# Fused attention and FFN layer: weight loads for the next head pair issued one pair earlier, V weights in two staging buffers

## The chip, the cores and the metric

The kernel runs on the 8 cores of one Trainium2 chip, each core with one of the 8 sequences of the batch. The metric is device microseconds of the slowest core, median of several runs.

## The reference

Each core computes one transformer layer on x of 4096 tokens by 1024 features: causal self-attention with 16 heads of 64, projection, residual and layer norm, then an FFN (1024 to 4096, exact GELU, back to 1024), residual and layer norm. Cut to what matters here:

```python
qkv = x @ c_attn_kernel.T + c_attn_bias          # c_attn_kernel: [3*1024, 1024], float32
q, k, v = jnp.split(qkv, 3, axis=2)              # then 16 heads of 64
scores = jnp.einsum('bqhd,bkhd->bhqk', q * scale, k) + causal_bias
attn = jnp.einsum('bhqk,bkhd->bqhd', softmax(scores), v).reshape(b, s, d)
x = layernorm(x + attn @ c_proj_kernel.T + c_proj_bias)
x = layernorm(x + gelu(x @ w1 + b1) @ w2 + b2)
```

## The kernel before

The program has three stages with a barrier between them: attention, projection with the first layer norm, FFN with the second. The change is in the first.

**Pairs and units.** Heads are worked on in 8 pairs (`NPAIR`). A pair's loop has 144 units: query tile g of 512 tokens (g from 0 to 7) against key block j of 128 tokens, 4(g+1) blocks for tile g. For a unit TensorE computes the scores of two heads (L762), ScalarE the exponential (L792; L808 for the four blocks on the diagonal, which VectorE then masks, L818), TensorE multiplies by V (L837). The scores of the next unit are issued ahead of this unit's product with V. At the end of a tile VectorE copies the sums out (L856), and the tile's tail begins: the row of softmax sums goes to DRAM and back into 128 partitions on SyncE's queue, VectorE takes the reciprocal (L711), it goes to DRAM again, GpSimd loads it as a broadcast (`rb<-r_s`) and multiplies (L736, L742). `flush_tail` places a tail two tiles later, and the last two at the end of the pair. After them stands the store of the pair's result (`attn_s<-arena`).

**The next pair's preparation.** While pair p-1 is computed, Q, K and V of pair p are prepared. `make_start(p)` builds a list of small pieces (thunks): load 128 rows of the Q and of the K weights with a cast from float32 to bfloat16 (`t_wld`, GpSimd's queue), transpose them on TensorE (`t_wtr`, L351) and copy them out (L359), then the Q and K projections (`t_qk`, L379, L389, L396) with a norm bound (`t_nrm`, L436, L449), and at last a bias column (`t_cb`, L498, L507). For even p the list goes on with V for the pairs p and p+1: two loads of 128 rows (`t_vld`), their transposes (`t_vtr`, L540) and copies (L548), and the V projection per key block (`mk_vg`, L562, L572, L579, copied out by L600 and L607). Odd pairs need no V work.

A thunk with a negative number is run as soon as it heads the list and takes no unit's place; of the others each unit from the ninth on takes one. So the Q and K loads of pair p are written into unit 0 of loop p-1, their transposes into units 8 and 9, and the V loads just ahead of their transposes, at about units 59 and 60. Loop 1 in the text below is the loop over pair 0, loop 2 that over pair 1, and so on.

**Order and waits.** Each engine executes its own instructions in the order in which this program adds them, and an instruction waits for the semaphores of what it depends on. GpSimd runs ahead of TensorE where nothing stops it: a load written just ahead of its transposes can be issued much earlier in time. Loads with a cast are issued by GpSimd alone. They land in `wcastA`, 3072 columns: two slabs of 1024 for Q and K, one for V, which the second V load (r = 1) can fill only once the first slab has been transposed and copied out:

```python
            def t_vld(r):
                stg = wcastA[:, 2048:3072]
                if r >= 1:
                    dep_stage = H_["vwtr"][r - 1]
```

**The prologue.** Before the first loop, x is loaded in 16 tiles of 256 tokens into two staging buffers (`xstage_b`, 4096 columns, not used afterwards), transposed on TensorE (L641) and copied into `xT` (L649); between them the thunks of pair 0 run as far as their numbers allow.

In the trace's names `arena` is the one large buffer in on-chip memory of which all of these are parts, `ps` is the accumulator memory, `wqkv` the Q, K and V weights in DRAM. DMAs of GpSimd all have line L239, those of SyncE L231.

Of the kernel before, what the change touches and what calls it, by code (L numbers as in the profile page):

```python
# [13 lines left out]
D = 1024  # L14
FF = 4096
NPAIR = 8
# [87 lines left out]
def build_nc(S=4096, debug_taps=False):  # L104
    NTG = S // TGA
    NKT = S // 128
    NTT = S // 128
# [5 lines left out]
    wqkv_d = nc.dram_tensor("wqkv", [3 * D, D], F32, kind="ExternalInput").ap()  # L113
# [120 lines left out]
    def gp_dma(stream, outs_ins, deps=(), tag=""):  # L234
        sem = sch._sem(stream)

        def em():
            for o, i in outs_ins:
                gp.dma_start(out=o, in_=i).then_inc(sem, 16)  # L239
        return sch.add("pool", em, deps, tag, n_dma=len(outs_ins), sem=stream)  # L240
# [45 lines left out]
    xstage_b = bf(A_xstage, 4096)  # L286
    last_ev = {0: None, 1: None}
    xT_ready = [None] * NTT

    xTb = xT  # L290
    wcastA = bf(A_wcast, 3072)
# [13 lines left out]
    qsq_user = [None, None]  # L305
    pending_vevs = {}
    handles = [None] * NPAIR

    def make_start(p):
        pb = p % 2  # L310
# [21 lines left out]
        thunks = []  # L332
# [3 lines left out]
        def t_wld(wi):  # L336
            row0 = [128 * p, D + 128 * p][wi]
            stg = wcastA[:, 1024 * wi : 1024 * wi + 1024]
            dep_stage = handles[p - 1]["wtr"][wi] if p > 0 else None
            ld = gp_dma(f"pw{wi}", [(stg, wqkv_d[row0 : row0 + 128, :])],  # L340
                        (dep_stage,), f"wld{p}.{wi}")
            H_["wld"].append(ld)

        def t_wtr(wi):
            wdstT = [H_["wqT"], H_["wkT"]][wi]
            stg = wcastA[:, 1024 * wi : 1024 * wi + 1024]
            bki = 4 + wi % 2
            def em_wtr(stg=stg, bki=bki):
                r = None
                for k in range(8):  # L350
                    r = t.transpose(  # L351
                        bank_bf(bki)[:, 128 * k : 128 * k + 128],
                        stg[:, 128 * k : 128 * k + 128],
                        idb,
                    )
                return r
            tr = sch.add("pe", em_wtr, (H_["wld"][wi], bank45_user[wi % 2]), f"wT{p}.{wi}")
            def em_wev(wdstT=wdstT, bki=bki):
                return v.tensor_copy(wdstT, bank_bf(bki)[:, 0:1024])  # L359
            ev = sch.add("dve", em_wev, (tr,), f"wTev{p}.{wi}")  # L360
            H_["wev"].append(ev)
            H_["wtr"].append(tr)
            bank45_user[wi % 2] = ev

        for wi in range(2):
            thunks.append((-1, lambda wi=wi: t_wld(wi)))
        for wi in range(2):
            thunks.append((0, lambda wi=wi: t_wtr(wi)))

        def t_qk(qi, g):  # L370
            wT = [H_["wqT"], H_["wkT"]][qi]
# [141 lines left out]

        thunks.append((NKT - 1, t_cb))

        if p % 2 == 0:
            wvg = bf(A_wvT, 2048)
            va_next = bf(A_va + ((p + 1) % 3) * 2 * 65 * NKT, 2 * 65 * NKT)
            va3_next = va_next.rearrange("p (h a c) -> p h a c", h=2, a=NKT, c=65)
            vevs_next = pending_vevs[p + 1]  # L520
            vstate = {"wld": []}

            def t_vld(r):
                row0 = 2 * D + 128 * p + 128 * r
                stg = wcastA[:, 2048:3072]
                if r >= 1:
                    dep_stage = H_["vwtr"][r - 1]
                else:
                    dep_stage = handles[p - 2]["vwtr"][1] if p >= 2 else None
                ld = gp_dma("pw2", [(stg, wqkv_d[row0 : row0 + 128, :])],  # L530
                            (dep_stage,), f"vwld{p}.{r}")
                vstate["wld"].append(ld)

            def t_vtr(r):
                stg = wcastA[:, 2048:3072]
                bki = 4 + r % 2
                def em_wtr(stg=stg, bki=bki):
                    rr = None
                    for k in range(8):
                        rr = t.transpose(  # L540
                            bank_bf(bki)[:, 128 * k : 128 * k + 128],
                            stg[:, 128 * k : 128 * k + 128],
                            idb,
                        )
                    return rr
                tr = sch.add("pe", em_wtr, (vstate["wld"][r], bank45_user[r % 2]), f"vwT{p}.{r}")
                def em_wev(r=r, bki=bki):
                    return v.tensor_copy(  # L548
                        wvg.rearrange("p (f pr c) -> p f pr c", f=8, pr=2, c=128)[:, :, r, :],
                        bank_bf(bki).rearrange("p (a c) -> p a c", a=8, c=128),  # L550
                    )
                ev = sch.add("dve", em_wev, (tr,), f"vwTev{p}.{r}")
                H_["vwtr"].append(ev)
                bank45_user[r % 2] = ev
# [39 lines left out]
            def mk_vg_b(a):  # L594
# [17 lines left out]
                bank45_user[par] = ev2  # L612
                vevs_next.append(ev2)

            thunks.append((-1, lambda: t_vld(0)))
            thunks.append((0, lambda: t_vtr(0)))
            thunks.append((-1, lambda: t_vld(1)))
            thunks.append((1, lambda: t_vtr(1)))
            for a in range(NKT):
                thunks.append((a, lambda a=a: mk_vg(a)))  # L620
                thunks.append((a, lambda a=a: mk_vg_b(a)))
# [4 lines left out]
    for tp_ in range(NTT // 2):  # L626
        b_ = tp_ % 2
        stg = xstage_b[:, 2048 * b_ : 2048 * b_ + 2048]
# [37 lines left out]
    for p in range(NPAIR):  # L666
        H_ = handles[p]
# [862 lines left out]
```

How the kernel before makes its waits and increments, by code:

```python
    def emit_engine(self, name, eng):  # L80
        sems = self.sems
        wm = {}
        for op in self.ops:
            if op.eng != name:
                continue
            for d in op.deps:
                if d.eng == "pe" and name == "pe":
                    continue
                v = d.val
                if wm.get(d.sem, 0) >= v:
                    continue
                eng.wait_ge(sems[d.sem], v)
                wm[d.sem] = v
            last = op.emit()
            if not op.is_dma:
                assert last is not None, f"op {op.tag} returned no instruction"
                last.then_inc(sems[op.sem], 1)
        if name == "pool":
            for sname, val in sorted(self.final.items()):
                if val > 0 and sname not in ("pe", "act", "dve"):
                    eng.wait_ge(sems[sname], val)
# [127 lines left out]
        def em():  # L229
            for o, i in outs_ins:
                sp.dma_start(out=o, in_=i).then_inc(sem, 16)
# [5 lines left out]
        def em():  # L237
            for o, i in outs_ins:
                gp.dma_start(out=o, in_=i).then_inc(sem, 16)
```

## Time and profile before

| | us |
|---|---|
| median of 3 runs | 3476.89 |
| lowest, highest of the 3 | 3474.47, 3582.14 |
| the profiled execution's own time | 3474.0 |
| its span on the slowest core (7) | 3472.5 |
| spans of cores 0, 1, 2, 3 | 3453.8, 3466.9, 3470.2, 3461.1 |
| spans of cores 4, 5, 6, 7 | 3454.7, 3471.2, 3458.3, 3472.5 |
| busy on core 7: TensorE, ScalarE | 2757.3, 1655.8 |
| busy on core 7: VectorE, GpSimd | 758.7, 305.6 |

The profiled execution is one run; its span goes from the first to the last instruction of the slowest core. Busy time is the sum over an engine's instructions, and a busy TensorE is not TensorE at its peak, since matmuls overlap in its pipeline. The attention loops lie at about 180 to 2120 us.

### The profile page before, as it was taken

How to read it: one execution, taken by the hardware profiler on the slowest of the kernel's cores; microseconds unless marked ns; L12 is line 12 of the kernel's file. 1: busy time of each engine (PE TensorE's matmuls, PEld its weight loads, DVE VectorE, ACT ScalarE, POOL GpSimd, SP SyncE). 2: the span in 40 equal slices, each digit the busy share in tenths (PEclk: the TensorE clock that was granted, in tenths of full speed). 3: DMA queues.
4: the chain of work that ended last, by engine and by line, in shares of the span. 5: the costliest groups of instructions: out<-in, count | busy, mean ns of one | idle time of the engine just before them, and what ended most of it. 6: DMA issues, size and time to landing. Idle time of an engine off the chain costs nothing.

```text
span 3472.5 us, 42144 instructions; the slowest of 8 cores (3453.8 to 3472.5 us)
## 1 busy us (share of the span) xinstructions
PE 2757.3 (79%) x14609; PEld 1222.6 (35%) x14609; DVE 758.7 (22%) x2136; ACT 1655.8 (48%) x1969; POOL 305.6 (9%) x383
## 2 busy tenths in 40 slices
PE   5687687888687787788787673577689999999997
PEld 2432123322123222223221111222456656566664
DVE  3442132232232242242231210233000000000000
ACT  0046745647655647546558783255133343433433
POOL 1000110010110110100111111111200000000000
PEclk9899998989898899899899996788899999999998
DMA  4200100010100100100100003865721111111110
GB/s 75 48 7 10 25 17 10 10 28 7 28 13 10 28 10 7 31 10 10 28 10 10 26 10 88 178 235 187 154 53 55 37 55 31 43 50 37 55 31 25
DMA packets 88204, 155.16 MB, mean 45 GB/s; under 512 B 26208, under 2 KB 50944, under 8 KB 85952
## 3 DMA queue, kind: packets, MB, share of 16 engines
q0 software_dynamic: 32736, 100.69, 11.6%
q1 hardware_dynamic: 55264, 51.78, 5.4%
q8 instruction: 124, 2.03, 0.2%
q14 instruction: 80, 0.66, 0.1%
HBM read 135.14 MB, written 50.86 MB: 54 GB/s over the span
## 4 chain that ended last, share of the span: by engine, by line
PE 62%; DMA 11%; ACT 9%; issue 9%; DVE 7%; POOL 1%; DVEq 0%; ACTq 0%; SPq 0%; POOLq 0%
PE ps L1306 12%; PE ps L1255 12%; PE ps L837 11%; ACT arena L792 7%; PE ps L762 7%; PE ps L389 4%; PE ps L379 3%; DMA arena<-x 3%; PE ps L974 3%; DMA arena<-w 2%; PE ps L572 2%; PE ps L562 2%; DMA rb<-r_s 2%; DMA arena<-wqkv 2%; PE ps L436 1%
## 5 line engine op out<-in xcount | busy, mean ns | idle before, releaser
L792 ACT ACTIVATE arena<-ps,cbt 128x1024 bf16<-128x1024 f32 x896 | 979.5, 1115 | 489.7 <-PE ps L762 488.5
L837 PE MATMUL ps<-arena 128*65 128x512 bf16 x2304 | 740.6, 405 | 221.2 <-DVE arena L818 90.6
L1255 PE MATMUL ps<-arena 128*128 128x256 bf16 x4096 | 539.6, 276 | 42.1 <-ACT arena L1276 23.6
L1306 PE MATMUL ps<-arena 128*128 128x512 bf16 x2048 | 532.7, 383 | 45.1 <-DVE stats L1368 28.1
L1276 ACT ACTIVATE arena<-ps,b1f 128x256 bf16<-128x256 f32 x512 | 238.8, 476 | 603.7 <-PE ps L1306 568.4
L1255 PEld LDWEIGHTS ps<-arena 128*128 128x128 bf16 x4096 | 402.7, 99 | 209.7 <-issue 60.7
L762 PE MATMUL ps<-arena 64*128 64x512 bf16 x2304 | 468.3, 404 | 0.0
L837 PEld LDWEIGHTS ps<-arena 128*65 128x65 bf16 x2304 | 183.3, 113 | 498.1 <-issue 467.6
L808 ACT ACTIVATE arena<-ps,cbt 128x1024 bf16<-128x1024 f32 (+3 forms) x256 | 200.5, 795 | 256.8 <-PE ps L762 256.8
L762 PEld LDWEIGHTS ps<-arena 64*128 64x128 bf16 x2304 | 110.4, 93 | 510.5 <-issue 510.4
L1306 PEld LDWEIGHTS ps<-arena 128*128 128x128 bf16 x2048 | 199.7, 99 | 190.4 <-issue 59.4
L1338 DVE SCALAR_TENSOR_TENSOR arena<-ps,arena 128x512 f32<-128x512 f32 x64 | 40.4, 688 | 919.0 <-PE ps L1316 919.0
L818 DVE TENSOR_TENSOR arena<-arena,masks_s 128x128 bf16<-128x128 bf16 x512 | 99.3, 234 | 611.1 <-ACT arena L808 595.5
L974 PE MATMUL ps<-arena 128*128 128x512 bf16 x512 | 136.4, 414 | 66.3 <-DVE arena L995 65.4
L239 POOL DMA_DIRECT2D rb<-r_s x64 | 35.7, 557 | 1570.9 <-DMA r_s<-rowf 1570.9
L416 DVE CAST arena<-ps 128x512 bf16<-128x512 f32 x128 | 88.6, 692 | 358.7 <-PE ps L396 358.7
L379 PE MATMUL ps<-arena 128*128 128x512 bf16 x512 | 140.4, 399 | 23.4 <-DVE arena L649 11.8
L389 PE MATMUL ps<-arena 128*128 128x512 bf16 x512 | 135.5, 388 | 0.0
L1019 ACT ACTIVATE arena<-arena 128x1024 f32<-128x1024 f32 x32 | 33.8, 1058 | 195.2 <-PE ps L1157 112.7
L436 PE MATMUL ps<-arena,ones_bf 128*1 128x512 bf16 x128 | 50.7, 396 | 95.9 <-DVE arena L427 95.9
L449 DVE TENSOR_REDUCE stats<-ps 1x1 f32<-1x512 f32 x128 | 86.9, 679 | 83.3 <-PE ps L436 83.3
L736 POOL TENSOR_TENSOR arena<-arena,rb 64x512 bf16<-64x512 f32 x64 | 80.4, 1256 | 203.6 <-DMA rb<-r_s 203.6
(96 smaller groups left out, 1582.5 us busy)
## 6 DMA issues: line engine op xcount, KB each, us to landing
rb<-r_s POOLq DMA_DIRECT2D x64, 256.0 KB, 3.6
arena<-x SPq DMA_DIRECT2D x8, 2048.0 KB, 10.9
x_s<-arena POOLq DMA_DIRECT2D x8, 2048.0 KB, 7.8
arena<-x_s SPq DMA_DIRECT2D x16, 1024.0 KB, 6.5
out<-arena POOLq DMA_DIRECT2D x16, 1024.0 KB, 8.5
arena<-x POOLq DMA_DIRECT2D x16, 512.0 KB, 7.1
attn_s<-arena POOLq DMA_DIRECT2D x8, 1024.0 KB, 5.2
arena<-attn_s SPq DMA_DIRECT2D x64, 128.0 KB, 11.1
```

What stands on the lines that cost most here:

```text
L379: r = t.matmul(bank(bki), wT[:, 128 * fc : 128 * fc + 128], xTb[:, S * fc + TGA * g : S * fc + TGA * g + TGA], start=(fc == 0), stop=False,)
L389: t.matmul(bank(bki), wT[:, 128 * fc : 128 * fc + 128], xTb[:, S * fc + TGA * g : S * fc + TGA * g + TGA], start=False, stop=False,)
L416: return v.tensor_copy(dst[:, TGA * g : TGA * g + TGA], bank(bki))
L762: r = t.matmul(PS[:, 1024 * ub + 512 * hh : 1024 * ub + 512 * hh + 512], k2[64 * hh : 64 * hh + 64, 128 * j : 128 * j + 128], q2[64 * hh : ...
L792: return sc.activation(Pb, quad, AF.Exp, bias=cbcol, scale=0.125)
L808: return sc.activation(Pb.rearrange("p (h c) -> p h c", h=2, c=512)[:, :, dcol:], quad.rearrange("p (h c) -> p h c", h=2, c=512)[:, :, dcol:],
L818: r = v.tensor_tensor(Pb[:, 512 * hh + dcol : 512 * hh + dcol + 128], Pb[:, 512 * hh + dcol : 512 * hh + dcol + 128], masks[:, 0:128], ALU ...
L837: r = t.matmul(PS[0:65, 3072 + 512 * hh : 3584 + 512 * hh], va[:, 65 * (NKT * hh + j) : 65 * (NKT * hh + j) + 65], Pb[:, 512 * hh : 512 * ...
L974: r = t.matmul(bank(bki), atg[:, TGA * fc + 128 * tc : TGA * fc + 128 * tc + 128], wpT[:, 1024 * fc + 512 * oh : 1024 * fc + 512 * oh + 51 ...
L1255: r = t.matmul(bank(bki)[:, 0:TGC], w1sb[:, FF * fc + 128 * hc : FF * fc + 128 * hc + 128], x2Tt[:, TGC * fc : TGC * fc + TGC], start=(fc ...
L1276: lambda hc=hc, hb=hb, htile=htile: sc.activation(htile, bank(F1BANKS[hb])[:, 0:TGC], AF.Gelu, bias=b1f[:, hc : hc + 1]),
L1306: r = t.matmul(bank(2 + 2 * tc + oh), htile[:, 128 * tc : 128 * tc + 128], w2sb[:, 1024 * hc + 512 * oh : 1024 * hc + 512 * oh + 512], sta ...
```

## The change

For Q and K, `t_wld` is now used for pair 0 alone. Every list puts, right behind the two transposes of its pair, two loads for the pair after it (`t_wld_next`) into the same two slabs; each waits for the transposes that read its slab. For V, the two loads of pairs 2, 4 and 6 are now written at the very head of the list before (`t_vld_next`, in the lists of pairs 1, 3 and 5), and go to the two halves of `xstage_b`, which is free after the prologue; they wait for the V transposes two pairs before to have been copied out. Pair 0's V loads stay as they were. TensorE's, VectorE's and ScalarE's instructions keep their order; only the buffers that L540 reads in pairs 2, 4 and 6 change.

```diff
         def t_wld(wi):
...
-            dep_stage = handles[p - 1]["wtr"][wi] if p > 0 else None
             ld = gp_dma(f"pw{wi}", [(stg, wqkv_d[row0 : row0 + 128, :])],
-                        (dep_stage,), f"wld{p}.{wi}")
+                        (), f"wld{p}.{wi}")
             H_["wld"].append(ld)
+
+        def t_wld_next(wi):
+            row0 = [128 * (p + 1), D + 128 * (p + 1)][wi]
+            stg = wcastA[:, 1024 * wi : 1024 * wi + 1024]
+            ld = gp_dma(f"pw{wi}", [(stg, wqkv_d[row0 : row0 + 128, :])],
+                        (H_["wtr"][wi],), f"wld{p + 1}.{wi}")
+            wld_pending[p + 1].append(ld)
...
-        for wi in range(2):
-            thunks.append((-1, lambda wi=wi: t_wld(wi)))
+        if p == 0:
+            for wi in range(2):
+                thunks.append((-1, lambda wi=wi: t_wld(wi)))
+        else:
+            H_["wld"] = wld_pending.pop(p)
         for wi in range(2):
             thunks.append((0, lambda wi=wi: t_wtr(wi)))
+        if p + 1 < NPAIR:
+            wld_pending[p + 1] = []
+            for wi in range(2):
+                thunks.append((-1, lambda wi=wi: t_wld_next(wi)))
...
+        if p % 2 == 1 and p + 1 < NPAIR:
+            vld_pending[p + 1] = []
+
+            def t_vld_next(r):
+                row0 = 2 * D + 128 * (p + 1) + 128 * r
+                stg = xstage_b[:, 1024 * r : 1024 * r + 1024]
+                if p + 1 == 2:
+                    dep = (handles[0]["vwtr"][1], xT_ready[NTT - 1])
+                else:
+                    dep = (handles[p - 1]["vwtr"][r],)
+                ld = gp_dma("pw2" if r == 0 else "pw3",
+                            [(stg, wqkv_d[row0 : row0 + 128, :])],
+                            dep, f"vwld{p + 1}.{r}")
+                vld_pending[p + 1].append(ld)
+
+            for r_ in (1, 0):
+                thunks.insert(0, (-1, lambda r=r_: t_vld_next(r)))
...
-            vstate = {"wld": []}
+            vstate = {"wld": [] if p == 0 else vld_pending.pop(p)}
...
             def t_vtr(r):
-                stg = wcastA[:, 2048:3072]
+                if p == 0:
+                    stg = wcastA[:, 2048:3072]
+                else:
+                    stg = xstage_b[:, 1024 * r : 1024 * r + 1024]
...
-            thunks.append((-1, lambda: t_vld(0)))
-            thunks.append((0, lambda: t_vtr(0)))
-            thunks.append((-1, lambda: t_vld(1)))
-            thunks.append((1, lambda: t_vtr(1)))
+            if p == 0:
+                thunks.append((-1, lambda: t_vld(0)))
+                thunks.append((0, lambda: t_vtr(0)))
+                thunks.append((-1, lambda: t_vld(1)))
+                thunks.append((1, lambda: t_vtr(1)))
+            else:
+                thunks.append((0, lambda: t_vtr(0)))
+                thunks.append((1, lambda: t_vtr(1)))
```

Where loads move, on GpSimd. In the prologue, the difference (rows with + are new); `arena<-x` are the tiles of x, `arena<-wqkv` slabs of weights, and the words in brackets the semaphores waited for (`sem_pe` TensorE, `sem_dve` VectorE):

```order
 L239 DMA arena<-x 128x2x1024 [waits sem_spc,sem_dve,sem_pbias,sem_pe]
 L239 DMA arena<-wqkv 128x1024 x2
+L239 DMA arena<-wqkv 128x1024 [waits sem_pe] x2
 L239 DMA arena<-x 128x2x1024
 L239 DMA arena<-x 128x2x1024 [waits sem_dve] x14
 L239 DMA arena<-wqkv 128x1024
```

The Q and K loads of pair 1 have moved ahead of the second tile of x, and wait there for TensorE's transposes of pair 0's slabs.

At the head of the second loop, and about its 60th unit, GpSimd before: the end of the tail of pair 0, the store, then the Q and K loads of pair 2; further down the two V loads, one on each side of a tile's tail:

```order
L742 TENSOR_TENSOR arena<-arena,rb 64x512
L239 DMA attn_s<-arena 128x4096 [waits sem_pool]
L239 DMA arena<-wqkv 128x1024 [waits sem_pe] x2
L239 DMA rb<-r_s 64x1024 [waits sem_sr0]
```

```order
L742 TENSOR_TENSOR arena<-arena,rb 64x512
L239 DMA arena<-wqkv 128x1024 [waits sem_dve]
L239 DMA rb<-r_s 64x1024 [waits sem_sr1,sem_pool]
L736 TENSOR_TENSOR arena<-arena,rb 64x512 [waits sem_pl1]
L742 TENSOR_TENSOR arena<-arena,rb 64x512
L239 DMA arena<-wqkv 128x1024 [waits sem_dve]
L239 DMA rb<-r_s 64x1024 [waits sem_sr0,sem_pool]
```

The same engine in the changed kernel, from the last loads of the prologue to the first tail of the first loop (the third row holds pair 0's second V load and pair 2's first):

```order
L239 DMA arena<-x 128x2x1024 [waits sem_dve] x14
L239 DMA arena<-wqkv 128x1024
L239 DMA arena<-wqkv 128x1024 [waits sem_dve] x2
L239 DMA arena<-wqkv 128x1024
L239 DMA arena<-wqkv 128x1024 [waits sem_pe] x2
L239 DMA rb<-r_s 64x1024 [waits sem_sr0]
```

Both V loads of pair 2 and its Q and K loads are now on the queue ahead of every tail of the first loop. In the second loop the place behind the store holds the Q and K loads of pair 3, and no V load stands among its tails.

## Rows read from the trace of the kernel before

**Rows 1.** The page, section 1: busy us (share of the span) xinstructions.

```profile
PE 2757.3 (79%) x14609; PEld 1222.6 (35%) x14609; DVE 758.7 (22%) x2136; ACT 1655.8 (48%) x1969; POOL 305.6 (9%) x383
```

**Rows 2.** List of waits, core 7: us in total, times, longest.

```profile
PE ps L540 <- DMA arena<-wqkv: 51.2, 4, 15.2
PE ps L351 <- DMA arena<-wqkv: 46.8, 7, 8.2
PE ps L641 <- DMA arena<-x: 10.4, 2, 8.9
```

**Rows 3.** Timeline, head of loop 2: start, us, engine, line, operation [idle before <-releaser].

```profile
413.76 1.03 PE L837 MATMUL ps<-arena 128*65 128x512 bf16 x2 [4.67 <-DVE arena L818]
...
425.28 1.26 POOL L742 TENSOR_TENSOR arena<-arena,rb 64x512 bf16<-64x512 f32 x1
...
427.69 1.09 POOL L239 DMA_DIRECT2D arena<-wqkv  x2
...
436.20 1.01 PE L351 MATMUL ps<-idb_s,arena 128*128 128x128 bf16 x8 [8.11 <-DMA arena<-wqkv]
...
445.07 1.22 DVE L856 COPY arena<-ps 65x1024 f32<-65x1024 f32 x1
```

**Rows 4.** Timeline, the two V loads and their transposes in loop 2.

```profile
513.54 0.60 POOL L239 DMA_DIRECT2D arena<-wqkv  x1
...
540.08 0.62 PE L540 MATMUL ps<-idb_s,arena 128*128 128x128 bf16 x8
...
553.59 0.60 POOL L239 DMA_DIRECT2D arena<-wqkv  x1
...
557.73 1.01 PE L540 MATMUL ps<-idb_s,arena 128*128 128x128 bf16 x8 [15.20 <-DMA arena<-wqkv]
...
560.24 1.12 ACT L792 ACTIVATE arena<-ps,cbt 128x1024 bf16<-128x1024 f32 x1 [16.48 <-PE ps L762]
```

**Rows 5.** Timeline, the transposes of the Q weights in loop 1.

```profile
201.47 0.62 PE L351 MATMUL ps<-idb_s,arena 128*128 128x128 bf16 x8
```

**Rows 6.** Stretches: us, busy of PE, PEld, DVE, ACT, POOL, granted clock, DMA share, GB/s.

```profile
420.40:428.10 7.70, 6.22 (x16) 1.17 (x16) 1.45 (x3) 4.29 (x4) 3.94 (x5) 0.56 0.12 37
436.10:441.00 4.90, 4.80 (x25) 2.35 (x26) 2.50 (x6) 0.69 (x1) 0.00 (x0) 0.50 0.03 6
540.90:542.50 1.60, 1.54 (x4) 0.29 (x4) 1.03 (x2) 0.47 (x1) 0.00 (x0) 0.50 0.01 5
557.70:561.30 3.60, 3.57 (x18) 1.91 (x18) 0.69 (x1) 1.06 (x1) 0.00 (x0) 0.52 0.02 5
1214.00:1450.00 236.00, 185.07 (x754) 51.21 (x754) 63.62 (x159) 146.55 (x144) 26.54 (x27) 0.91 0.06 17
2200.00:2450.00 250.00, 151.93 (x751) 61.96 (x749) 76.71 (x274) 108.98 (x136) 43.14 (x78) 0.79 0.66 205
2450.00:3472.00 1022.00, 931.05 (x6208) 607.09 (x6208) 60.53 (x272) 361.28 (x672) 26.87 (x46) 0.97 0.19 50
```

**Rows 7.** Timeline, the prologue's loads and transposes, and pair 0's second V transposes.

```profile
9.03 0.74 POOL L239 DMA_DIRECT2D arena<-x  x1 [5.80 <-DVE b1f L280]
...
10.84 0.73 POOL L239 DMA_DIRECT2D arena<-x  x1
...
16.99 1.86 PE L641 MATMUL ps<-idb_s,arena 128*128 128x128 bf16 x16 [8.95 <-DMA arena<-x]
...
21.90 1.01 PE L351 MATMUL ps<-idb_s,arena 128*128 128x128 bf16 x8 [2.12 <-DMA arena<-wqkv]
...
24.37 1.87 PE L641 MATMUL ps<-idb_s,arena 128*128 128x128 bf16 x16 [1.46 <-DMA arena<-x]
...
143.89 1.01 PE L540 MATMUL ps<-idb_s,arena 128*128 128x128 bf16 x8 [5.68 <-DMA arena<-wqkv]
```

**Rows 8.** List of waits, core 2.

```profile
PE ps L540 <- DMA arena<-wqkv: 50.3, 4, 15.2
PE ps L351 <- DMA arena<-wqkv: 41.2, 8, 7.0
```

More of the change, by code:

```diff
@@ L307, in build_nc @@
     handles = [None] * NPAIR
+    wld_pending = {}
+    vld_pending = {}
     def make_start(p):
@@ L525, in t_vld @@
                 stg = wcastA[:, 2048:3072]
[L526 to L529, printed above, removed]
+                dep_stage = H_["vwtr"][r - 1] if r >= 1 else None
                 ld = gp_dma("pw2", [(stg, wqkv_d[row0 : row0 + 128, :])],
```

## The prediction, made before the changed kernel was run

> **What bounds the kernel now.** I read the page first, then the list of waits, then the timeline around each wait that the change touches, then granted clock by stretch, then the cores. The page's first section has TensorE busy for 79% of the span and no other engine above 48% [rows 1]; TensorE executes strictly in the order written, so while it waits no attention work is done. The question is how much of its idle time hangs on the weight loads that the change moves. The list of waits answers: the transposes of the V weights (L540) waited 51.2 us for `arena<-wqkv` in 4 waits, those of the Q and K weights (L351) 46.8 us in 7 waits [rows 2]. The change can touch only these 98.0 us.
>
> Where do they lie? The program has 8 pairs of heads, and each loop over a pair also prepares the next. For Q and K the timeline of the second loop shows it: GpSimd normalises the last tile of the previous pair (L742, from 425.28), issues the store of that pair's result, and only then the two loads, at 427.69. TensorE waits 8.11 us, from about 428.1, and starts the transposes at 436.20 [rows 3]. So these loads are late because they stand on GpSimd's queue behind the tail of the previous pair, not because the data would be slow. In the first loop, which has no earlier pair, the same transposes begin at 201.47 with no wait [rows 5]: this is what the changed kernel should look like in all loops. For V the first of two loads was issued at 513.54, 26 us ahead, and its transposes at 540.08 did not wait. The second waits for the first one's buffer and stands behind a normalisation; it is issued at 553.59, lands 4.1 us later, and TensorE has stood 15.20 us. ScalarE stood beside it, 16.48 us until the next scores came [rows 4]. Nothing else filled the gap, so the stalls are on the path.
>
> **The change part by part.** The sum is made against the profiled run, 3474.0 us (span 3472.5 on core 7, 1.5 around it). The median of the three runs shown is 3476.9, 2.9 above it.
>
> Early Q/K loads, loops 2 to 7. The program's 7 waits of L351 hold one in the prologue, 2.12 us [rows 7], which stays, since that load is not moved. The other six are 46.8 - 2.1 = 44.7 us. In the changed kernel these loads are issued a whole pair earlier (some 235 us), behind transposes that are done by then: -44.7.
>
> Early V loads, pairs 2, 4, 6. Of the 4 waits of L540 the first, 5.68 us at 143.89 [rows 7], belongs to pair 0 and stays (its load goes out as before, with less behind it; I count nothing, since a load alone took 4.1 us too [rows 4]). The other three are 51.2 - 5.7 = 45.5 us. They go whole, since each V slab now has a buffer of its own: -45.5. Next late after the second transposes is VectorE's copy of them, as before; 0 to 3 us over three places, taken as 0.
>
> TensorE's clock. In the stretch behind the Q/K stall, 436.1 to 441.0, TensorE was granted 0.50 of its clock, that is 1.2 instead of 2.4 GHz, with 4.80 us busy; behind the V stall, 557.7 to 561.3, 0.52 with 3.57 us busy [rows 6]. At the full clock that work takes half: 2.4 us saved in each of six places and 1.8 in each of three, 19.8 in all, if the clock is full there once the stalls are gone. Against it: it was already at 0.56 in 420.4 to 428.1, ahead of the stall, and at 0.50 in 540.9 to 542.5 [rows 6]. So the low stretch would partly only move. Bounds 0 and -20; I take the middle, -10.
> The Trainium skill, TensorE: Matmul & The Clock Gate (Part 1: The HAM clock gate), says that the throttled clock is the default and that only activity lifts it, which makes all of the slow work behind a stall a cost of the stall. By that rule the sum has -20 here. The trace agrees that a stall is followed by the low level, but also shows the low level in a stretch where TensorE was busy 6.22 of 7.70 us.
>
> Cost in the prologue. The two Q/K loads of pair 1 now stand on GpSimd's queue ahead of the second tile of x, and wait for the transposes of pair 0's weights. Before, the second x load was issued at 10.84 and its transposes started at 24.37. Now it can go only after the transposes that start at 21.90 and take 1.0, plus 0.6 for issuing the last weight load: at 23.5. All 14 later x loads are queued behind it, and TensorE's next work behind x. The first x load took 9.03 to 16.99, 7.96 us, with nothing ahead of it [rows 7]: 23.5 + 7.96 - 24.37 = +7.1. Lower bound: in a filled queue x came only about 2.5 us after the weight load ahead of it (21.90 to 24.37), 23.5 + 2.5 - 24.37 = +1.6. Upper: that 2.5 once more for the weight load now just ahead, +9.6. I take +7. It cannot be a gain. The later x loads have time to catch up: only two of the 16 were ever waited for, the first and the second [rows 2, 7].
> The Trainium skill, DMA: Bandwidth & Descriptors (Anatomy of one DMA), puts a load at about 2 us plus its bytes at 436 GB/s. For 1 MB of x that is an estimated 4.4 us and the term would be +3.5. The row has 7.96 for the same load, and the row is used.
>
> In the loops, the moved loads' waits block GpSimd only until the transposes of the same loop; what stands behind them is the first tile's 1/sum broadcast, which waits for its own chain anyway: 0.
>
> The slowest core. Core 7 loses the most from these waits, 98.0 us; core 2 has 91.5 [rows 8], with a span of 3470.2 against 3472.5. If its prologue parts are like core 7's, core 2 ends at 3470.2 - (91.5 - 7.8) = 3386.5 before the other terms, core 7 at 3472.5 - 90.2 = 3382.3. The end may pass to core 2: bounds 0 and +4, taken +3.
>
> Sum: 3474.0 - 44.7 - 45.5 - 10 + 7 + 3 = 3383.8, so 3384 us, 2.7% below the median before.
>
> **The rivals.**
> 1. The clock comes back whole (-20 for -10): 3374. For it: the low level stands right behind each stall. Against: it is also there ahead of two of them.
> 2. A new wait takes the place: with TensorE 8 us earlier at the head of a pair, it meets the tail of the previous one. The next such need is VectorE's copy of the second tile (L856, at 445.07), which needs the normalisation that ended at 426.54; it would come at about 437, 10 us too late to wait [rows 3]. For it: at 413.76 TensorE did stand 4.67 us in such a tail [rows 3]. If each of six loops gave that back: 3384 + 28 = 3412, no change by the measurement.
> 3. The prologue costs more, since x stays behind and the clock falls there too: twice the upper bound, +19 instead of +7: 3396.
> 4. Slower: denser work on all cores lowers the granted clock of the attention loops. In 1214 to 1450 it was 0.91 with TensorE busy 185 of 236 us; in 2200 to 2450, another stage, 0.79 [rows 6]. Estimated over the 1812 us from 138 to 1950 that is 1421 us busy; at 0.79 they would take 15% more, +216, so 3600. It decides below 0.854, where 93 us of gain are used up. Against it: the last stage is denser still, 931 of 1022 us, and was granted 0.97 [rows 6].
> 5. The loads are early but TensorE still waits, because the wait was for something else. Against: the first V load, issued early, had no wait [rows 4]. It would give 3474 + 7 = 3481.
>
> **How the numbers follow.** Forecast 60%, rival 1 15%, rival 2 8%, rival 3 11%, rival 4 2%, rival 5 4%. Low end: 3474.0 - 90.2 - 20 + 2 = 3366, high end: 3474.0 - 90.2 + 0 + 10 + 4 + 3 (copies) = 3401, plus the 2.9 between the profiled run and the median and a little of rival 2: 3405. A measurement of this kernel can tell 2% from no change, which is 3407. Forecast, rivals 1 and 3 lie beyond it, 86%, and a part of rival 2: 0.87 faster; the rest of rival 2 and rival 5, 0.11 the same; rival 4, 0.02 slower.
>
> **What would show it.** In the profile after, the waits of L351 and L540 for `arena<-wqkv` should fall from 98.0 to about 8 us (the prologue's only), in 2 or 3 waits; loops 2 to 7 should each be about 8 us shorter, those with V work about 23. The start of the second x transposes should move from 24.37 to about 31. If granted clock right behind the old stall places is full, the clock term is nearer to 20. I am wrong if TensorE waits at the heads of pairs for L856 or L818 grow by more than 10 us in sum, if the prologue grows by more than 10 us, or if the mean granted clock of the loops falls below 0.90.

## The result and the profile after

The changed kernel takes 3389.85 us (median of 10 runs, 3385.48 to 3520.88), the kernel before 3480.06 us (median of its 10, 3474.47 to 3739.96). The ratio is 0.9743, with a 95% interval of 0.9732 to 0.9754, so 2.6% faster. The forecast was 3384, range 3366 to 3405. Some executions, here and in most runs below, were disturbed on one die; the ratios leave them out, and the medians do not.

The cores of the profiled execution, 3389.8 us:

```profile
core 0: 3375.9 us, clock 0.931
core 1: 3388.3 us, clock 0.932
...
core 7: 3365.2 us, clock 0.936
```

The slowest is now core 1. Core 7, from which the rows before the prediction come, is 107.3 us shorter than before, core 1 only 78.6 (3466.9 before). Where that spread comes from is told below. The page's first section, of core 1, has TensorE busy for less time and a larger share than in [rows 1]:

```profile
PE 2738.3 (81%) x14609; PEld 1214.1 (36%) x14609; DVE 760.0 (22%) x2136; ACT 1653.5 (49%) x1969; POOL 305.1 (9%) x383
```

The same 14609 matmuls are busy for 19 us less, on another core and with the clock at 0.932 for 0.920.

The line numbers have moved: L351 is now L359, L540 is L573, L641 is L678, L818 is L855, L856 is L893, L742 is L779. The list of waits of core 7 (us in total, times, longest), which answers [rows 2]:

```profile
PE ps L678 <- DMA arena<-x: 18.7, 2, 9.4
PE ps L573 <- DMA arena<-wqkv: 5.4, 1, 5.4
DVE arena L893 <- POOL arena L779: 10.0, 7, 2.5
```

Of 98.0 us of waits for weights 5.4 are left, in one wait, the one of pair 0's second V load. The transposes of Q and K weights have none at all. The second tile of x is waited for longer (18.7 in both waits, 10.4 before). The third line was 6.5 us in 4 waits before: VectorE's copy of the sums meets the tail of the pair before a little more often.

The head of the second loop on core 7, start, us, operation [idle before], which answers [rows 3]:

```profile
422.50 1.04 PE L874 MATMUL ps<-arena 128*65 128x512 bf16 x2 [4.65 <-DVE arena L855]
...
433.68 1.26 POOL L779 TENSOR_TENSOR arena<-arena,rb 64x512 bf16<-64x512 f32 x1
...
435.26 0.62 PE L359 MATMUL ps<-idb_s,arena 128*128 128x128 bf16 x8
435.50 0.61 POOL L239 DMA_DIRECT2D attn_s<-arena  x1 [0.55 <-POOL arena L779]
...
442.62 1.22 DVE L893 COPY arena<-ps 65x1024 f32<-65x1024 f32 x1
```

The tail of pair 0 takes as long as before and TensorE still stands 4.65 us in it. But the transposes now start at 435.26, before GpSimd has even issued the store, and run for 0.62 us instead of 1.01. L893 comes at 442.62, 7.7 us after that normalisation ended, and does not wait.

The V transposes in the second loop, which answer [rows 4]:

```profile
539.11 0.62 PE L573 MATMUL ps<-idb_s,arena 128*128 128x128 bf16 x8
...
541.49 1.03 PE L573 MATMUL ps<-idb_s,arena 128*128 128x128 bf16 x8
```

Between the two it was 17.65 us before, of which 15.20 were the stall; now it is 2.38. The second ones still run at the low clock, as did the work just ahead of them before. Stretches of core 7 (us, busy PE, PEld, DVE, ACT, POOL, granted clock, DMA share, GB/s), to be held against [rows 6]:

```profile
435.20:440.00 4.80, 4.21 (x32) 1.82 (x30) 3.48 (x11) 2.42 (x4) 1.67 (x3) 1.00 0.70 230
541.40:545.00 3.60, 3.56 (x22) 1.68 (x20) 1.81 (x3) 2.12 (x2) 0.00 (x0) 0.72 0.02 2
1152.00:1378.00 226.00, 180.05 (x759) 49.78 (x760) 64.01 (x159) 147.09 (x145) 27.78 (x30) 0.95 0.08 20
```

The work at the Q/K transposes, 0.50 before, is at the full 2.4 GHz. At the V transposes TensorE is back at it within the stretch. The last line is the loop that took 236 us at 0.91: now 226 at 0.95, with 180.05 us busy for 185.07. Measured on core 7 from one pair's Q transposes to the next one's, the loops without V work are 8.3 to 10.7 us shorter than before and the three with it 24.5 to 27.7, where about 8 and 23 had been expected.

The prologue, which answers [rows 7]:

```profile
18.66 1.91 PE L359 MATMUL ps<-idb_s,arena 128*128 128x128 bf16 x16
...
20.26 0.53 POOL L239 DMA_DIRECT2D arena<-wqkv  x1 [9.66 <-PE ps L359]
21.11 0.53 POOL L239 DMA_DIRECT2D arena<-wqkv  x1 [0.32 <-issue]
21.63 1.43 POOL L239 DMA_DIRECT2D arena<-x  x2
30.01 1.86 PE L678 MATMUL ps<-idb_s,arena 128*128 128x128 bf16 x16 [9.44 <-DMA arena<-x]
```

GpSimd waits 9.66 us in front of the first moved load. Only then, at 21.63, does it issue the second tile of x (10.84 before), and its transposes start at 30.01 instead of 24.37.

**By stage.** Single cores differ by more than the smaller terms, so I divide the program by two instructions that every core has, and take the mean over the 8 cores. VectorE's copies of the sums (L856, now L893) begin and end the loops; the first FFN matmul (L1255, now L1292) begins the last stage. Each boundary is read from the first and last start in a line like this one, of core 7 after:

```profile
L893 DVE COPY arena<-ps x64: 1207/1221/1222, 202.0 to 2020.3; 65x1024 f32<-65x1024 f32 x64
```

| mean of 8 cores, us | first copy at | loops | middle stage | last stage | span |
|---|---|---|---|---|---|
| before | 193.2 | 1920.5 | 327.5 | 1022.5 | 3463.6 |
| after | 199.6 | 1823.8 | 329.0 | 1022.5 | 3374.9 |
| after, once more (below) | 200.0 | 1822.0 | 323.7 | 1022.3 | 3368.1 |

The prologue costs 6.4 us, the loops give back 96.7. The last stage is as before; the middle one differs by 1.5 us, and by 3.8 in the second execution, with no instruction of it changed.

### The profile page after: what moved, and what is told of

Read it like the earlier page. It is cut to its first block, busy times and chain, and to the rows that moved or that the text cites. A ratio compares the mean times of both kernels' runs of the same rounds, so it can differ in the third digit from the quotient of the medians.

```text
span 3388.3 us, 42148 instructions; the slowest of 8 cores (3364.1 to 3388.3 us)
## 1 busy us (share of the span) xinstructions
PE 2738.3 (81%) x14609; PEld 1214.1 (36%) x14609; DVE 760.0 (22%) x2136; ACT 1653.5 (49%) x1969; POOL 305.1 (9%) x383
## 4 chain that ended last, share of the span: by engine, by line
PE 63%; ACT 10%; issue 9%; DMA 9%; DVE 8%; POOL 0%; DVEq 0%; ACTq 0%; SPq 0%; POOLq 0%
PE ps L1343 12%; PE ps L1292 12%; PE ps L874 12%; ACT arena L829 8%; PE ps L799 7%; PE ps L404 4%; PE ps L394 4%; DMA arena<-x 4%; PE ps L1011 3%; DMA arena<-w 2%; PE ps L605 2%; PE ps L595 2%; DVE arena L442 2%; DVE arena L855 1%; PE ps L451 1%
## 5 line engine op out<-in xcount | busy, mean ns | idle before, releaser
L874 PE MATMUL ps<-arena 128*65 128x512 bf16 x2304 | 731.9, 400 | 226.6 <-DVE arena L855 90.2
L1292 PE MATMUL ps<-arena 128*128 128x256 bf16 x4096 | 537.6, 275 | 47.1 <-ACT arena L1313 28.5
L1292 PEld LDWEIGHTS ps<-arena 128*128 128x128 bf16 x4096 | 401.8, 99 | 213.2 <-issue 64.4
L1375 DVE SCALAR_TENSOR_TENSOR arena<-ps,arena 128x512 f32<-128x512 f32 x64 | 40.4, 687 | 921.7 <-PE ps L1353 921.7
L855 DVE TENSOR_TENSOR arena<-arena,masks_s 128x128 bf16<-128x128 bf16 x512 | 97.1, 230 | 608.0 <-ACT arena L845 592.3
```

The lines of the kernel that those rows point to most:

```text
L855: r = v.tensor_tensor(Pb[:, 512 * hh + dcol : 512 * hh + dcol + 128], Pb[:, 512 * hh + dcol : 512 * hh + dcol + 128], masks[:, 0:128], ALU ...
L874: r = t.matmul(PS[0:65, 3072 + 512 * hh : 3584 + 512 * hh], va[:, 65 * (NKT * hh + j) : 65 * (NKT * hh + j) + 65], Pb[:, 512 * hh : 512 * ...
L1292: r = t.matmul(bank(bki)[:, 0:TGC], w1sb[:, FF * fc + 128 * hc : FF * fc + 128 * hc + 128], x2Tt[:, TGC * fc : TGC * fc + TGC], start=(fc ...
```

## The experiments

The loops' length as a mean over the cores turned out to be the sharpest measure: it is 1920.5 and 1919.0 in two kernels that should be equal in the loops, and 1822.0 to 1825.5 in five executions of kernels that should be equal there. So I take a difference of 5 us in it as clear of the noise, while a whole run moves by more than that. Each run below was compared with the kernel before on the same chip.

### Each part alone

**The Q/K part without the V part.** The diff against the changed kernel takes `t_vld_next` out and puts the old `t_vld` and its order back:

```diff
-            vstate = {"wld": [] if p == 0 else vld_pending.pop(p)}
+            vstate = {"wld": []}
...
-                dep_stage = H_["vwtr"][r - 1] if r >= 1 else None
+                if r >= 1:
+                    dep_stage = H_["vwtr"][r - 1]
+                else:
+                    dep_stage = handles[p - 2]["vwtr"][1] if p >= 2 else None
...
```

> Only the Q/K loads are moved; the V loads are as before. My theory (each stall is gone with its load, and the low clock behind it partly): the six waits of the Q/K transposes go, 44.7 us, with about 6 us of clock, against 6 us more in the prologue: 3477 - 45 = about 3432, ratio 0.987; the V transposes still wait about 51 us in 4 waits. Rival (the tail of the previous pair takes the wait's place): less than half of it comes, 3455 or more, and the waits for the masks (L818's place) or for the sums' copy at the heads of loops grow by over 10 us in sum.

Measured: 3436.99 us, ratio 0.9889 (0.9874 to 0.9905), loops 1872.7 (-47.8), first copy at 200.8. On core 7 the V transposes waited 51.5 us and the Q/K ones not at all. As my theory said, within 5 us.

**The V part without the Q/K part.** The diff against the kernel before adds only `t_vld_next`, its two halves of `xstage_b` and the new order of V thunks.

> Only the V loads of pairs 2, 4 and 6 are moved, to two buffers of their own a pair ahead; Q/K as before, the prologue too. My theory: 45.5 us of waits go with about 5 us of clock, nothing is added: 3477 - 50 = about 3427, ratio 0.985; the second x transposes start at about 24 us again. If the parts of the change add up, this gain and that of the Q/K loads alone make the 90 us of the whole. Rival (parts overlap): their sum is over 100 or under 80.

Measured: 3438.99 us, ratio 0.9901 (0.9865 to 0.9938), loops 1880.1 (-40.4). That is 9 us less than expected in the loops, and the two parts alone make 88.2 where the whole made 96.7. The timeline of core 7 shows where it went. The loads of the third loop's head, and the Q transposes there (L352 in this kernel) and in the two loops beside it:

```profile
432.81 1.01 PE L352 MATMUL ps<-idb_s,arena 128*128 128x128 bf16 x8 [6.10 <-DMA arena<-wqkv]
...
681.43 2.15 POOL L239 DMA_DIRECT2D arena<-wqkv  x4
...
690.73 1.01 PE L352 MATMUL ps<-idb_s,arena 128*128 128x128 bf16 x8 [9.60 <-DMA arena<-wqkv]
...
926.00 1.01 PE L352 MATMUL ps<-idb_s,arena 128*128 128x128 bf16 x8 [7.06 <-DMA arena<-wqkv]
```

In loops 1, 3 and 5 the V loads that the next loop will use stand at the head of the list, ahead of the Q/K loads that TensorE wants eight units later. Four loads go out together, and the urgent pair comes second: 9.60 and, in the fifth loop, 9.90 us of wait, where the next but one run below has 6.80 and 6.61 on the same core. In the mean over the 8 cores the six waits add up to 49.0 us here and to 41.6 in that run, which is 7.4 of the 9 us; the rest is within the noise. In the whole change the Q/K loads are no longer urgent there, so this costs nothing. The V loads' own waits were gone here too, but for pair 0's 5.7 us.

### The buffer or the place on the queue

**A buffer of its own for the second V load, same place.**

```diff
+                elif r == 0:
+                    deps = (handles[p - 2]["vwtr"][1],)
+                else:
+                    stg = xstage_b[:, 0:1024]
+                    sem = "pw3"
+                    deps = (xT_ready[NTT - 1], handles[p - 2]["vwtr"][1])
...
```

> The second V load of pairs 2, 4 and 6 gets a buffer of its own and no longer waits for the first slab, but stays where it stands on GpSimd's queue, behind a tile's tail. My theory (the place on the queue is the cause): nothing changes, ratio 1.000, and the load is still issued about 11 us after TensorE has reached its transposes, with three waits of about 15 us. Rival (the shared buffer is the cause): the waits go, 3427, ratio 0.985.

Measured: ratio 0.9993 (0.9981 to 1.0005), loops 1919.0. Nothing changed. The load and its transposes on core 7:

```profile
553.40 0.60 POOL L239 DMA_DIRECT2D arena<-wqkv  x1
557.40 1.01 PE L545 MATMUL ps<-idb_s,arena 128*128 128x128 bf16 x8 [14.86 <-DMA arena<-wqkv]
```

It is issued at 553.40 where the kernel before issued it at 553.59 [rows 4], though nothing in the data holds it any more. Only the tile's tail ahead of it on GpSimd does: its last multiply begins there at 552.20.

**The same, and written right behind the first V load.** Further to the last diff:

```diff
...
+                thunks.append((-1, lambda: t_vld(0)))
+                thunks.append((-1, lambda: t_vld(1)))
+                thunks.append((0, lambda: t_vtr(0)))
+                thunks.append((1, lambda: t_vtr(1)))
```

> As the run with the buffer alone, but the second V load is also written right behind the first, ahead of that tail; nothing is a pair ahead. My theory: GpSimd issues both about 26 us before the transposes, the three waits of 15 us go: about 3427, ratio 0.985, like the V loads a whole pair ahead. Rival (only loads a pair ahead are early enough, since DMA traffic delays them): waits of some us remain and the time lies between 3435 and 3477.

Measured: 3429.79 us, ratio 0.9858 (0.9837 to 0.9879), loops 1871.2 (-49.3). GpSimd issues both at once, and only pair 0's wait is left:

```profile
144.09 1.01 PE L545 MATMUL ps<-idb_s,arena 128*128 128x128 bf16 x8 [7.20 <-DMA arena<-wqkv]
...
512.77 1.14 POOL L239 DMA_DIRECT2D arena<-wqkv  x2
```

So the whole V gain is to be had without loading a pair ahead, and 9 us better than in the V part alone, since these loads meet nothing urgent. Together with the Q/K part's 47.8 it makes 97.1, which is the 96.7 of the whole. The parts add up.

### What the Q/K stall is made of

**The store behind the loads**, in the kernel before: the call that stores the pair's result is put off until the next loop's two loads are written.

```diff
             while nxt_i < len(nxt) and nxt[nxt_i][0] < 0:
                 nxt[nxt_i][1]()
                 nxt_i += 1
+            while store_due:
+                store_due.pop(0)()
...
```

> The kernel before, with one thing swapped: the 1 MB store of a pair's result is issued behind the two Q/K loads at the head of the next loop instead of ahead of them. The loads stay behind the tail of the previous pair. My theory (a part of the Q/K stall is the store that fills the DMA queues ahead of the loads: 8.5 us from issue to landing against 4.1 for a weight load alone): each of the six waits falls from 7.5 to about 4 us, in all about -20 us and a little clock: 3477 - 22 = 3455, ratio 0.994. Rival (the store costs nothing, the loads alone take 8 us): waits stay at 7 us, ratio 0.999 to 1.001.

Measured: ratio 0.995 (0.9933 to 0.9967), loops 1906.9 (-13.6). The six waits on core 7 add up to 28.8 us for 44.7; the issue of the first two loads, the first wait and the last:

```profile
427.93 1.15 POOL L239 DMA_DIRECT2D arena<-wqkv  x2
433.50 1.01 PE L352 MATMUL ps<-idb_s,arena 128*128 128x128 bf16 x8 [4.84 <-DMA arena<-wqkv]
...
1714.00 1.01 PE L352 MATMUL ps<-idb_s,arena 128*128 128x128 bf16 x8 [3.79 <-DMA arena<-wqkv]
```

A third of the Q/K stall was the 1 MB store ahead of the loads. In the mean over all 48 such places on the 8 cores the wait fell from 6.9 to 4.3 us. The time from the loads' issue to the first transposes fell from 6.6 to 5.1 us, and the issue itself came 1.2 us sooner against TensorE's arrival; 0.6 of that is the store's own issue, which GpSimd no longer makes first. So a little over half of this third is faster landing, the rest the earlier issue. What is left is a load that GpSimd issues, behind the tail, only as TensorE arrives; no run took the tail alone away. I had expected 20 us of waits, 16 came.

### The clock behind a stall

**The stalls filled**, in the kernel before: useless matmuls ahead of the transposes that wait, into the accumulator bank that these overwrite. The diff shows those for Q; the V ones are alike, with 48.

```diff
+            if p >= 2 and wi == 0:
+                def em_fill(bki=bki):
+                    r_ = None
+                    for k in range(12):
+                        r_ = t.matmul(bank(bki), xTb[:, 0:128], xTb[:, 0:512],
+                                      start=True, stop=True)
+                    return r_
+                sch.add("pe", em_fill, (bank45_user[wi % 2],), f"fill{p}.{wi}")
...
```

> The kernel before, with matmuls of no use put ahead of the transposes that wait: 12 ahead of each Q one in loops 2 to 7 (5 us at the low clock) and 48 ahead of each second V one of pairs 2, 4, 6 (10 to 14 us, partly at the low clock), so TensorE is busy where it stood. My theory (the low clock behind a stall is a cost of the stall): the work behind the stalls runs at the full clock and the attention loops get 5 to 11 us shorter though no wait for a load ends sooner; the mean over cores of the loops' length, 1920.5 us before, falls to 1910 to 1915. Rival (the low clock there has other causes, such as the short waits ahead of it): loops as long as before, 1919 to 1922, or longer where the filling overruns a wait.

Measured: ratio 1.0002 (0.9992 to 1.0012), loops 1922.2. Taken by itself that speaks for the rival. But the filling had been too short. Two places on core 7:

```profile
544.19 11.43 PE L558 MATMUL ps<-arena 128*128 128x512 bf16 x48
559.65 1.01 PE L548 MATMUL ps<-idb_s,arena 128*128 128x128 bf16 x8 [4.03 <-DMA arena<-wqkv]
...
1729.51 0.61 PE L351 MATMUL ps<-idb_s,arena 128*128 128x128 bf16 x8 [3.19 <-DMA arena<-wqkv]
1731.03 1.03 PE L351 MATMUL ps<-idb_s,arena 128*128 128x128 bf16 x8
```

TensorE ran nearly all of the filling at the full clock (11.43 us for 48 matmuls is 0.24 each), then still stood 3 to 6 us. At seven of the nine places on core 7, the V one shown among them, the transposes behind began slow, 1.01 us for eight. At the other two, of which 1729.51 is one, the first eight were fast (0.61) and the next eight slow (1.03), so there the clock fell as the work behind went on. The run did not remove what it was to remove, so it decides nothing.

**Filled longer**: 26 for 12 and 62 for 48 matmuls.

> As stalls_filled, with 26 useless matmuls ahead of each Q transpose and 62 ahead of each second V one. There TensorE still stood 3 to 6 us at the end of each wait, and most of the work behind began at 0.5 of the clock again. Now 1 us or less should be left of each wait. My theory: the transposes behind then take 0.62 us instead of 1.01, with the clock granted in full, and the loops' mean length falls from 1920.5 to about 1910 to 1915, less what the filling overruns. Rival: the clock is low behind the waits although TensorE was busy, or it is full and the loops are still 1919 us or longer without an overrun.

One profiled execution and one round, so no interval; its 8 cores give loops of 1905.5 us, 15.0 less than before. Its time is 3469.14 us, for a median of 3477.51 of the kernel before on that chip: of the 15 us only 8 reach the slowest core, whose middle stage took 338.6 us where the mean before was 327.5. The first Q place and the second V place in the timeline of core 7:

```profile
422.32 5.80 PE L361 MATMUL ps<-arena 128*128 128x512 bf16 x26
...
428.56 0.61 PE L351 MATMUL ps<-idb_s,arena 128*128 128x128 bf16 x8 [0.44 <-DMA arena<-wqkv]
...
1046.57 0.61 PE L548 MATMUL ps<-idb_s,arena 128*128 128x128 bf16 x8 [0.59 <-DMA arena<-wqkv]
```

The stretches behind the first place of each kind, with the columns of [rows 6]:

```profile
428.50:433.40 4.90, 4.46 (x32) 1.99 (x32) 3.64 (x11) 1.17 (x2) 0.00 (x0) 1.00 0.06 11
547.60:551.20 3.60, 3.39 (x25) 1.71 (x25) 0.69 (x1) 1.69 (x2) 0.00 (x0) 1.00 0.00 0
```

The loads are issued where they were and TensorE's own work has to wait for them as before, with useless work in front: from its last useful matmul to the transposes the nine places take 86.0 us in the mean over the cores, for 86.6 before. Yet the loops are 15 us shorter, and the 4.9 and 3.6 us behind the waits are at 1.00 instead of 0.50 and 0.52 [rows 6]. The low clock there is a cost of the stall, and in all nine places together it is worth about 15 us, by this one execution. This is what the rule in the Trainium skill, TensorE: Matmul & The Clock Gate (Part 1: The HAM clock gate), says, that activity lifts the throttle and idling sets it; the trace agrees, 0.50 for 1.00.

### The prologue, and a version that beats both

**The changed kernel once more**, as measure for the two behind it.

> The changed kernel once more, as the measure for the two below on the same chip: ratio 0.974, about 3390.

Measured: 3380.11 and 3381.33 us in its two lowest executions. The kernel before took 3475.0 on this chip (mean of its four lowest), which makes 0.973, without an interval. So the changed kernel came out some 9 us faster here than the 3390 taken as measure, and the runs below have to be held against 3381. Its profile gave the third row of the table of stages.

**x first**: the Q/K loads of pair 1 are written behind all x loads.

```diff
-            for wi in range(2):
-                thunks.append((-1, lambda wi=wi: t_wld_next(wi)))
+            if p > 0:
+                for wi in range(2):
+                    thunks.append((-1, lambda wi=wi: t_wld_next(wi)))
...
+        if p == 0:
+            for wi in range(2):
+                thunks.append((NKT - 1, lambda wi=wi: t_wld_next(wi)))
         thunks.append((NKT - 1, t_cb))
```

> The changed kernel, with the Q/K loads of pair 1 written behind all loads of x in the prologue instead of ahead of the second. My theory (they delay the second x load by the time GpSimd waits for the weight transposes): the second x transposes start at 24 us instead of 30, all that follows comes 6 us earlier, 3390 - 6 = 3384, and the first loop's Q/K transposes of pair 1 still do not wait. Rival (the 6 us are lost again at the wait for pair 0's V load or in the later stages): no difference, 3390.

Measured: ratio 0.9722 (0.9703 to 0.9741), first copy at 194.1 for 199.6 and 200.0, loops 1823.2. The second x transposes start at 21.73 on core 7, and the Q/K ones of pair 1 do not wait. The prologue's 6 us come back with the order alone. In the whole time they can't be told from noise: the interval overlaps that of the changed kernel, and on this chip its three lowest executions average 3378.5 for 3381.

**And pair 0's second V load early too**, into space that the loops use only later. The diff leaves out the transposes that read this space, and the order: `t_vld(1)` now stands right behind `t_vld(0)`.

```diff
-                stg = wcastA[:, 2048:3072]
-                dep_stage = H_["vwtr"][r - 1] if r >= 1 else None
-                ld = gp_dma("pw2", [(stg, wqkv_d[row0 : row0 + 128, :])],
-                            (dep_stage,), f"vwld{p}.{r}")
+                stg = wcastA[:, 2048:3072] if r == 0 else bf(A_u, 1024)
+                ld = gp_dma("pw2" if r == 0 else "pw3",
+                            [(stg, wqkv_d[row0 : row0 + 128, :])],
+                            (), f"vwld{p}.{r}")
...
```

> As the run with x first, and pair 0's second V load gets a buffer of its own (space that the loops use only later) and is issued right behind the first. My theory: the last wait for a weight load, 5.4 us at about 144 us, goes, with up to 1 us of clock: 3384 - 6 = 3378, ratio 0.971. Rival: the two loads now share the DMA queues with the two Q/K loads issued just ahead, and a wait of 2 to 5 us remains.

Measured: ratio 0.9718, with a wide interval (0.9657 to 0.9779). No wait for V weights is left on core 7. From the first matmul of pair 0's `t_cb` to the first copy it is 54.3 us on six cores, 59.5 before this edit; on the other two the prologue ran at 0.72 and 0.74 of the clock from 25 us on, for a reason that the trace does not show. So I ran it again:

> The version with x first and both V loads of pair 0 early, once more for its interval: by my theory 6 us of prologue and 5 us at pair 0's V load better than the changed kernel, 3390 - 11 = 3379, ratio 0.971. Rival: as the changed kernel, 0.974.

Measured: ratio 0.9706 (0.9691 to 0.9721), first copy at 188.6, loops 1822.5. This is the best version. It reaches the first copy 11 us sooner than the changed kernel, as expected. In the whole time it is 0.4% ahead of 0.9743, the intervals apart, but measured on two chips; against the 0.973 of the changed kernel's second run it is 0.2%, so how much of the 11 us the slowest core keeps stays open.

**The last tail deferred.** What stalls TensorE next at the heads of the loops is the 4.65 us behind L855. It comes from VectorE, which at a pair's end waits for the last tile's sums to return from DRAM, with the masks queued behind. This edit to the best version puts that tail and the store behind the fourth unit of the next loop:

```diff
+            if ui == 4 and end_due:
+                end_due.pop(0)()
...
-        while pending_tail:
+        while len(pending_tail) > 1:
             flush_tail()
...
```

> The best version so far (x first, both V loads of pair 0 early), and the tail of a pair's last tile with the pair's store is written behind the fourth unit of the next loop, so VectorE no longer waits at the end of a pair for the sums' way through DRAM with the next masks behind it. My theory: the 4.65 us wait of TensorE at the head of each of loops 2 to 8 goes, 7 x 4.65 = 33 us, with up to 10 us of clock: 3380 - 35 = 3345, ratio 0.962. Rival (the copy of the sums of the second tile then waits for the late normalisation): half or less comes, 3360 to 3380, and the copy's waits for GpSimd grow from about 10 to over 25 us.

Measured: ratio 0.973 (0.9712 to 0.9747), loops 1836.6, which is 14 us longer than in the best version. The rival was right, and more than right. The timeline of core 7 at the head of the second loop, the first tile's copy (L900 here) and TensorE behind it:

```profile
415.91 1.26 POOL L784 TENSOR_TENSOR arena<-arena,rb 64x512 bf16<-64x512 f32 x1
417.27 1.22 DVE L900 COPY arena<-ps 65x1024 f32<-65x1024 f32 x1 [5.89 <-POOL arena L784]
...
418.63 1.03 PE L881 MATMUL ps<-arena 128*65 128x512 bf16 x2 [6.20 <-DVE rowf L753]
```

The list of waits of the same core:

```profile
PE ps L881 <- DVE rowf L753: 60.9, 23, 8.1
DVE arena L900 <- POOL arena L784: 47.0, 10, 7.8
```

The copy reuses one of three buffers, which the tail before the last must have read. The copy now comes sooner and stands 5.89 us for that tail, and TensorE behind it 6.20, more than the 4.65 that were removed. This copy's waits went from 11.2 us in the best version to 47.0. So the stall at the pair's end hid a longer one.

## Why the prediction was right

**The early Q/K and V loads: -44.7 and -45.5.** Right. All nine waits are gone. Of the two others pair 0's 5.68 is 5.4, and the prologue's 2.12 is gone as well, with the second tile of x no longer issued beside these loads. The sum of the nine was 82.9 to 90.2 us by core, 86.6 in the mean (each core's rows like those of [rows 3] and [rows 4] added up), so core 7's rows gave 3.6 us more than the mean core had. That the queue and not the buffer held the second V load was an explanation only; the two buffer runs show it.

**The clock: -10, from 0 to -20.** Right in size: the loops are 96.7 shorter, which is 86.6 of waits and 10.1 more. That the middle of the two bounds was hit so closely is luck, and the reason for taking it was partly wrong. I held the low clock ahead of the stalls against the rule. With the stalls filled the cost of the low clock was about 15. The changed kernel gets less, and its rows show two places where it may go: at the V transposes it is still at 0.72, with the low level begun ahead of them as it was before the change, and the copies at the heads wait 3.5 us more. No run takes either away. The clock's return was seen where it was expected, 0.50 to 1.00.

**The prologue: +7, from +2 to +10.** Right: +5.6 at the second x transposes on core 7, +6.4 at the first copy in the mean. Two misses cancel in part. The issue came at 21.63 instead of the 23.5 that I worked out from the weight transposes at 21.90. Those were late in that execution: in the ten other profiled executions with the old order they start at 17.5 to 21.8 on core 7, always after a wait for the load, and in the three with the new order there is no wait. The tile then took 8.4 us from its issue to its transposes, and up to 9.5 in the two other executions with this order, for the 7.96 taken. By the fit of the Trainium skill, DMA: Bandwidth & Descriptors (Anatomy of one DMA), an estimated 4.4 us for such a load, the term would have been +3.5, half of the one taken. The measurement decides; that load had two weight loads ahead of it, which the figure does not count.

**The slowest core: +3, from 0 to +4.** The size was near, the reason was wrong. I derived the term from how much each core had waited for weights. Core 2 was to be the slowest; it came out at 3374.8, and core 1 at 3388.3. The spread is made elsewhere: the middle stage takes 321 to 338 us on the 8 cores after, and on one and the same core it changes between executions. On core 1 it took 325 us before, 338 after and 318 in the second profile of the changed kernel; on core 7 336, 324 and 320. The slowest core lost 84.2 us where the mean lost 88.7, so the term was +4.5 in this execution. What makes the middle stage vary I have not tested.

**The sum.** The profiled run is 3389.8 for the 3384 forecast. Of the 6 us, 3.6 are core 7's waits taken for every core's, 1.5 the middle stage and 1.5 the slowest core, with 0.6 the other way from the prologue. The first and the third are one mistake in part: the sum started from the core with the most waits, and then added something for the others. The second profile of the changed kernel, 3381.3, lies on the other side of the forecast, so that a closer hit than some 5 us would have been chance.

**The rivals.** The clock did not come back whole (rival 1), by the 10.1 above. A new wait in place of the old (rival 2) came only as the 3.5 us of copies: the 10 us of distance that I had worked out were 7.7. The deferred tail shows that the mechanism is real one step further on. The prologue stayed under rival 3's +19, and no wait for early loads was left for rival 5. The granted clock did not fall (rival 4): in the loop shown it rose from 0.91 to 0.95, and over all loops and cores in the mean from 0.92 to 0.95.

## What to carry to other kernels

On an engine that issues DMAs and also computes, as GpSimd does here, a load is as early as the last thing ahead of it on that queue, not as its data allows (issue at 553.40 for 553.59 with a buffer of its own). Look at its issue time beside the moment when it is wanted, and move its place before giving it buffers. When moving loads early, check at both ends what they are moved in front of: here two of them delayed the second tile of x by 6 us, and V loads alone lengthened the waits for the Q/K loads of two loops by 3 us each. Before removing a wait at a seam, look for the chain that ends just behind it; it may be longer than the wait.

## What the runs showed of the hardware

A stall of TensorE cost more than its length: in the run that filled nine stalls with useless matmuls the loops were 15 us shorter, with the clock behind at 1.00 instead of 0.50. A partial filling was worth nothing (loops 1922.2 for 1920.5): with 3 to 6 us left of each wait, most of the work behind ran at 1.2 GHz again. A 1 MB store issued just ahead of two 0.5 MB weight loads lengthened the wait for them by 2.7 us in the mean of 48 places, 1.5 of them between issue and first use. On one and the same core the middle stage, whose instructions no run changed, took from 318 to 338 us in three executions.
